# A graph network's edge table: zeroing and first scatters moved into the table stage, gathers paced otherwise

## The reference

```python
# attention: k, q, v per node by node type; per edge by edge type
a = (rel(k[src], rel_att, etype) * q[dst]).sum(-1) * rel_pri.T[etype] / sqrt(D)
ex = exp(a - segment_max(a, dst)[dst]);  attn = ex / segment_sum(ex, dst)[dst]
h = segment_sum(rel(v[src], rel_msg, etype) * attn, dst)
h = typed_linear(h, Wa, ntype) * gate + x * (1 - gate);  x = ln(x + ln(x + h) * gamma + beta)
# then three times, with the normalised weights norm of the edges:
h = x @ W;  agg = segment_sum(h[src] * norm, dst);  h = relu(batch_norm(agg + b))
```

## Time and profile before

| | |
|---|---|
| median of 3 runs | 4593.5 us (4591.87 to 4594.39) |
| the profiled execution | 4592.2 us, its span 4590.3 us |
| PE busy | 2969.0 us (65%) |
| DVE busy | 2312.5 us (50%) |
| POOL busy | 2411.3 us (53%) |
| ACT busy | 1147.0 us (25%) |
| table stage | start to about 405 us |
| attention, first gather to the last batch's logits less maxima (L1318) | 409 to 2168 us |
| first gather of the first convolution | 2595 us |

### The profile page before, as it was taken

One profiled execution on the slowest core, in us unless ns is written; L12 is line 12 of the kernel. 1 busy time (PEld: TensorE's weight loads), 2 busy tenths in 40 slices (PEclk: granted clock), 3 DMA queues, 4 the chain that ended last, 5 costly groups with the idle time before them and its releaser, 6 DMA issues. The chain is left out here.

```text
span 4590.3 us, 52237 instructions
## 1 busy us (share of the span) xinstructions
PE 2969.0 (65%) x14449; PEld 2143.5 (47%) x14449; DVE 2312.5 (50%) x8186; ACT 1147.0 (25%) x2512; POOL 2411.3 (53%) x2514
## 2 busy tenths in 40 slices
PE   3895666666676666664420666777767776767774
PEld 3774656666666656663200433344433444433342
DVE  3774655655655555553522345533455534455435
ACT  1223556555655555552001200000000000000001
POOL 0002544444466666665577266665466664666662
PEclk9998778777787877776755889988899988999987
DMA  4896555565422322221000455555545545555552
GB/s 110 273 358 232 199 200 210 189 216 191 163 88 80 87 79 81 84 81 48 1 1 0 172 190 174 189 191 184 186 174 190 189 174 179 192 188 176 189 189 61
DMA packets 232026, 706.47 MB, mean 154 GB/s; under 512 B 62326, under 2 KB 111957, under 8 KB 212928
## 3 DMA queue, kind: packets, MB, share of 16 engines
q1 hardware_dynamic: 104252, 447.79, 26.7%
q0 software_dynamic: 93184, 191.21, 14.4%
q10 hardware_dynamic: 34308, 64.13, 4.3%
HBM read 559.66 MB, written 143.28 MB: 153 GB/s over the span
## 5 line engine op out<-in xcount | busy, mean ns | idle before, releaser
L552 POOL DMA_INDIRECT stage<-h_tab,earr x1248 | 1183.3, 948 | 810.8 <-issue 346.5
L527 POOL DMA_INDIRECT arena<-kv_tab,idxr x832 | 796.0, 957 | 970.3 <-ACT idxr L634 405.6
L1013 PE MATMUL bank<-arena,xr 128*128 128x512 f32 (+1 forms) x2058 | 1021.1, 638 | 5.6 <-issue 5.6
L992 PE MATMUL bank<-oh,stage 128*128 128x128 f32 x2496 | 394.3, 308 | 494.0 <-issue 487.8
L992 PEld LDWEIGHTS bank<-oh,stage 128*128 128x128 f32 x2496 | 354.1, 214 | 712.3 <-issue 701.1
L860 PE MATMUL bank<-xr,arena 128*128 x3328 | 494.0, 308 | 236.8 <-DVE arena L1254 146.9
L1572 DVE TENSOR_TENSOR sums<-sums,bank 128x128 f32 x1248 | 351.3, 282 | 568.3 <-remote 398.2
L1013 PEld LDWEIGHTS bank<-arena,xr 128*128 128x128 f32 x2058 | 407.6, 212 | 394.8 <-issue 394.8
L860 PEld LDWEIGHTS bank<-xr,arena 128*128 128x128 f32 x3328 | 456.0, 218 | 259.3 <-issue 258.2
L499 POOL DMA_INDIRECT a_tab<-tot,cell x416 | 416.0, 1000 | 261.2 <-DMA arena<-kv_tab,idxr 151.1
L709 ACT ACTIVATE rs<-mv,epsc 128x49 f32<-128x49 f32 (+1 forms) x6 | 1.9, 316 | 2003.3 <-DVE mv L1611 1692.6
(11 more groups left out here) (224 smaller groups left out, 2739.4 us busy)
## 6 DMA issues: line engine op xcount, KB each, us to landing
arena<-a_tab SPq DMA_DIRECT2D x147, 1792.0 KB
a_tab<-stage SPq DMA_DIRECT2D x49, 1792.0 KB
kv_tab<-stage SPq DMA_DIRECT2D x48, 768.0 KB, 8.5
arena<-key_d ACTq DMA_DIRECT2D x52, 512.0 KB, 7.1
arena<-ew_d ACTq DMA_DIRECT2D x52, 512.0 KB, 10.1
arena<-rel_d SPq DMA_DIRECT2D x52, 512.0 KB
stage<-h_tab,earr POOLq DMA_INDIRECT x1248
arena<-kv_tab,idxr POOLq DMA_INDIRECT x832
```

The source lines that it names most:

```text
L527: G.indirect_dma_start(kv[b % 3][:, t, :], None, kv_tab, bass.IndirectOffsetOnAxis(idxr[:, b % 3, t:t + 1], 0))\
L552: G.indirect_dma_start(gring[:, (q % NG) * GRP + s, :], None, h_tab[l], bass.IndirectOffsetOnAxis(src_i[:, t:t + 1], 0)).then_inc(row_land ...
L992: last = M.matmul(bank[q % NG][:, s * P:(s + 1) * P], gring[:, (q % NG) * GRP + s, :], oh[:, q % NG, s, :], start=True, stop=True)
L1013: mm = M.matmul(o_[:, 0:cw], xr[:, n, :], abuf[B % NBUF][:, n % KB, 0:cw], start=n == 0, stop=n == NT - 1)
```

## The change

`a_tab` is zeroed by POOL in the table stage, from `hd`, a zeroed buffer of the sums that the attention needs later: 49 DMAs with rows of 14,336 bytes, released over the first 30 of the 49 node tiles. Then POOL waits for all zeros and issues the first 140 scatters; before every fourth it waits for all earlier ones to have landed. Only then does it wait for `tabs_complete` and begin to gather. SP's zero writes and the scatters between the gathers are gone. After the attention, 48 scatters come as before, then 228 instead of 224. The waits between gathers are changed: each group, the first of a batch too, waits for three of the four DMAs of the group before it (48), and for the fourth of the group before that (`kv_last`). DVE waits for the zeros before it clears `exw`.

```diff
+ZT = 30
+ST = 140
-                if b == 1:
-                    sp.wait_ge(zero_set, 2)
-                if b >= 1:
-                    for z in range(zeros_by(b - 1), zeros_by(b)):
-                        sp.dma_start(a_flat[z, :, :].rearrange("p (a f) -> p a f", a=4),
-                                     zero.rearrange("p (a f) -> p a f", a=1).to_broadcast([P, 4, ZW]))\
-                          .then_inc(a_zeroed[z // BPC], 16)
...
+            pool.wait_ge(zero_set, 1)
+            for z in range(NBLK):
+                if z:
+                    pool.wait_ge(kv_copied, z * ZT // NBLK)
+                G.dma_start(a_flat[z, :, :], hd[:, 0:KB * 512]).then_inc(a_zeroed[z // BPC], 16)
+            for j in range(ND):
+                pool.wait_ge(a_zeroed[j], 16 * BPC)
+            pool.wait_ge(cell_ready, 1)
+            for t in range(ST):
+                if t % GRP == 0:
+                    pool.wait_ge(cells_saved, 16 * t)
+                    pool.wait_ge(tot_added, KT * (t // KT + 1))
+                scatter(t)
             pool.wait_ge(tabs_complete, 1)
...
                 for g in range(NG):
-                    if g:
-                        pool.wait_ge(kv_land[b % 3][g - 1], 64 * (b // 3 + 1))
-                    for t in slots.get((b, g), ()):
-                        scatter(t)
+                    n = NG * b + g
+                    if n:
+                        b_, g_ = (n - 1) // NG, (n - 1) % NG
+                        pool.wait_ge(kv_land[b_ % 3][g_], 48 * (b_ // 3 + 1))
+                    if n >= 2:
+                        pool.wait_ge(kv_last[n % 2], 16 * (n // 2))
...
-                         .then_inc(kv_land[b % 3][g], 16)
+                         .then_inc(kv_land[b % 3][g] if s < GRP - 1 else kv_last[n % 2], 16)
...
-            V.memset(zero, 0.0).then_inc(zero_set, 1)
+            dve.sem_inc(zero_set, 1)
+            for j in range(ND):
+                dve.wait_ge(a_zeroed[j], 16 * BPC)
             V.memset(exw[:, :, :], 0.0).then_inc(exw_zero, 1)
```

More of the change, by code:

```diff
@@ L98, in gnn @@
     assert NT % KB == 0 and 2 * T1 == ET and T1 <= 512 and 512 * (ND - 1) < WD and WA + TPB <= 512 * ND and GT % GRP == 0
-    assert HALF + WD <= NW and T1 % KT == 0 and zeros_by(SB - 3) == NBLK
+    assert HALF + WD <= NW and T1 % KT == 0
     def groups_before(d):
@@ L247, in gnn @@
         a_zeroed = [sem(f"a_zeroed{j}") for j in range(ND)]
-        ZW = KB * 512 // 4
-        zero = stage[:, :, :, :].rearrange("p a r f -> p (a r f)")[:, TPB * P:TPB * P + ZW]
         edge_saved = [sem(f"edge_saved{a}") for a in range(2)]
@@ L263, in gnn @@
         kv_land = [[sem(f"kv_land{a}_{g}") for g in range(NG)] for a in range(3)]
+        kv_last = [sem(f"kv_last{a}") for a in range(2)]
         rel_in = [sem(f"rel_in{a}") for a in range(2)]
@@ L500, in scatter @@
                  .then_inc(cells_saved, 16)
-            pool.wait_ge(tabs_complete, 1)
[L504 to L508, removed]
+            pool.wait_ge(zero_set, 1)
[11 more added lines that the diff above has]
+                scatter(t)
+            pool.wait_ge(tabs_complete, 1)
             def gather(b):
@@ L528, in gather @@
                                              bass.IndirectOffsetOnAxis(idxr[:, b % 3, t:t + 1], 0))\
-                         .then_inc(kv_land[b % 3][g], 16)
+                         .then_inc(kv_land[b % 3][g] if s < GRP - 1 else kv_last[n % 2], 16)
             for b in range(NB):
                 gather(b)
-            for t in range(first_of, first_of + SY):
+            pool.wait_ge(tot_ready, 1)
+            for t in range(ST, ST + SY):
                 scatter(t)
@@ L537, in _ @@
             G.tensor_tensor(xr[:, :, :], xr[:, :, :], lnw[:, 1:2, :].to_broadcast([P, NT, D]), ALU.add).then_inc(xb_ready, 1)
-            for t in range(first_of + SY, T1):
+            for t in range(ST + SY, T1):
                 scatter(t)
@@ L632, in indices @@
                     for g in range(NG):
-                        act.wait_ge(kv_land[b % 3][g], 64 * (b // 3))
+                        act.wait_ge(kv_land[b % 3][g], 48 * (b // 3))
+                    for a in range(2):
+                        act.wait_ge(kv_last[a], 16 * (NG // 2) * (b - 2))
                 S.activation(idxr[:, b % 3, :], idx_c[:, bass.ds(b * TPB, TPB)], ACT.Copy).then_inc(idx_ready, 1)
@@ L1238, in _ @@
             dve.wait_ge(tabs_complete, 1)
[L1239 removed]
+            dve.sem_inc(zero_set, 1)
+            for j in range(ND):
+                dve.wait_ge(a_zeroed[j], 16 * BPC)
             V.memset(exw[:, :, :], 0.0).then_inc(exw_zero, 1)
             def products(b, i, par, g):
[L1244 removed]
+                dve.wait_ge(kv_land[b % 3][g], 48 * (b // 3 + 1))
+                dve.wait_ge(kv_last[g % 2], 16 * ((NG * b + g) // 2 + 1))
                 dve.wait_ge(q_done, NG * b + g + 1)
```

5 lines of the change are left out of this document (removed).

## The result

The changed kernel is a little slower: 4606.1 us median of 13 runs (4592.7 to 4621.4) against 4590.5 of the kernel before (13 runs, 4580.3 to 4594.9), a ratio of 1.003 with a 95% interval of 1.0021 to 1.004. Two later measurements gave 1.0043 (1.0019 to 1.0066) and 1.0033 (1.0019 to 1.0047). The profiled execution of the changed kernel took 4592.7 us, span 4591.0; it is the shortest of its 13. The forecast was 4505.

What follows compares the result with a forecast made beforehand. POOL's gathers and their landing waits were taken to bound the attention. A gain of 409 us there less 321 us lost before the first gather gave -88 us on 4592.2, so 4505 us; range 4425 to 4625.

Steps and rivals of the forecast that it cites:

- What bounds before: Attention of the kernel before: POOL bounds, sixteen gathers and three landing pauses making 27.1 us a plain batch.
- Part 1: Attention: without zeros and scatters, batches fall from 31.85 and 33.78 to 27.05 us, 277 us off POOL's path.
- Part 2: Attention: shorter waits between gathers bring a batch to 24.7 us; the attention gains 409 us in all.
- The pace: POOL's gathers in the attention: a group takes 6.07 us, all four of a batch 24.3 us.
- The three loops: Attention: the batch loops of DVE, ACT and POOL lie between 23.3 and 24.5 us, so 24.7 a batch.
- First batch: Start of the attention: 54.3 us less 6 for four shorter groups, 48 us.
- Last batch: End of the attention: 75.6 us before; its unexplained excess of 41.9 us over a batch is kept, giving 66.6.
- Part 3: Table stage: the zeros land at 455 us, the 29th tile copy comes at 443, the stage ends at 585 instead of 405.
- Part 4: Before the first gather: 140 scatters, 10 us a group beside full queues, then 6.6; first gather at 730, 321 us lost.
- Part 5: The rest of the kernel: SP's dropped DMAs and four more late scatters change nothing; all that follows shifts as it is.
- Rival 1: Attention: hand-offs between DVE, ACT and PE hold a batch at 27.05 us; gain 290 against 321 lost, 4625 us; chance 0.14.
- Rival 4: Attention: a batch takes 24.0 us and the last batch's stall goes, 4428 us; chance 0.08.

Runs made afterwards that it cites:

- e1: The changed kernel with the old waits between gathers (all four of the group before, none before a batch's first group): 4359.4 us, 1.0047 of before.
- e4: The changed kernel with the 48 scatters behind the last gather issued in fours, each after the landing of the earlier ones: 4311.4 us, 0.9939 of before.
- g2: The changed kernel with its 48 tail scatters in fours, without the gathers of batches 3 to 51 and the waits for them: 4412.2 us (one run).
- g4: The changed kernel unedited, run again beside a before of 4569.4 us: 4585.1 us, 1.0033 of before.
- after: The changed kernel as it is: 4606.1 us, 1.003 of before.
- f2: The changed kernel with its 48 tail scatters in fours and waits for all four gathers in the first three batches: 4586.9 us, 0.9992 of before.
- f1: The changed kernel with its 48 tail scatters in fours (the program of e4), beside a before of 4589.9 us: 4563.9 us, 0.9949 of before.
- g3: The kernel before with only its last 48 scatters issued in fours, each after the landing of the four before: 4534.1 us, 0.9929 of before.
- g1: The changed kernel with its 48 tail scatters in fours and groups waiting for two of four gathers, not three: 4966.7 us, 1.0873 of before.

## Why the prediction was wrong

The direction was wrong, by one term: the 24.7 us a batch, which were 25.6. Taken in the prediction's order:

- **What bounds before.** Right. POOL's pauses set 27.05 us a plain batch; e1 has 27.3 with the old waits and nothing else.
- **Part 1** (27.05 a batch without zeros and scatters). Right by e1.
- **Part 2, 24.7 us a batch. This step failed.** It stood on two terms, and both were too small.
  - The pace: "With the same 3.57 us it releases the next group". Most groups did (6.0 to 6.2 us), but one in six took over 7.2, so a batch of gathers takes 25.9 to 26.2 us instead of 24.3. I took one timeline of one group, with none of SP's loads beside it, for the mean. On kind B the same waits took a batch from 27.3 (e1) to 26.2 (e4).
  - The three loops: "between 23.3 and 24.5". They take 23.4 in g2, but only without POOL. Beside its gathers they take 25.0 to 25.7 on kind A (g4, after) while POOL has a lead. That they would need the same beside denser gathers was assumed without a reason.
  - Which of the two binds differs. In the profiled changed kernel it is the loops: DVE waits once, for 0.7 us, for gathered rows between 840 and 2060 us. In g4 it is first the loops and then the pace, on kind B the pace. Either alone keeps a batch at 25 us or more.
  - The missing 86 us can be put down either way, not both. By POOL's queue they are 52 batches of 1.6 us. By the other engines they are 25 in the first batch, 44 in the next 49 and 18 in the last two. A kernel near its sum's zero can't bear that: 409 earned against 321 paid left 88.
- **First batch**, 48: it took 73.1 on kind A and 43 on kind B. POOL's gathers go on meanwhile; f2 took the 20 us out by slowing POOL, and ended later.
- **Last batch.** "I have no cause for it; those scatters stand in the same place after, so I keep the excess." The excess stayed, and its cause on kind A was that row of 48 scatters (f1, g3). On kind B the same row costs nothing (17.0 us in e1).
- **Part 3.** Right: 29th tile copy 442.4 (443), first scatter 465.1 (455), last tile copy 578.9. The Trainium skill (DMA: Bandwidth & Descriptors, Specifications) gives 358 GB/s as the limit of device memory for a core; two slices of the page are above it, at 413 and 403, and the stretch from 75 to 470 us has 361. The trace doesn't bear it out as a limit for this kernel, and the measured packet prices were the better guide. The same page of the Trainium skill (Bandwidth, Measured) gives this figure for two cores of a pair that stream at once and 425 GB/s for one alone; this kernel runs on one core, and what the other did isn't on record.
- **Part 4.** Right in sum: first gather 740.9 (730), thirteen groups of 8.1 to 11.8 us beside full DMA queues, 10.4 on average (10), and mostly 6.2 where DMA is idle (6.6). Two of them, the gap ahead of each:

```profile
540.53 0.96 POOL L489 DMA_INDIRECT a_tab<-tot,cell  x1 [5.46 <-DMA a_tab<-tot,cell]
```

```profile
671.30 0.96 POOL L489 DMA_INDIRECT a_tab<-tot,cell  x1 [1.43 <-DMA a_tab<-tot,cell]
```

- **Part 5.** Nearly right: the rest of the kernel came 8.5 us shorter.
- **Rival 1** was the near one. It had the pace at 27.05 and 4625 us; it came to 25.9. Its point of decision was given as 26.5 us a batch, but that was reckoned by the batches alone. By POOL's pace it lies near 26: 24.3 plus 88/52. Its reason, the hand-offs by themselves, was wrong (g2). Rival 4's other half, that the last batch's stall goes, did not come: on kind A that needs the 48 scatters spread (f1), not the other 140 moved.

## What to carry to other kernels

A pause that looks like waste on a queue can be what lets another engine work. Before taking pauses out, look for an engine whose instructions come slowly with nothing to wait for while the queue's row is close, and try the row in both densities. And a period that is multiplied by fifty must come from the mean of many groups, not from one timeline, and must be read beside what the other queues move once in each period: here 1 to 1.6 us a batch turned a gain of 2% into none.

## What the runs showed of the hardware

- On kind A TensorE's matmuls come 0.7 or 1.4 us apart instead of 0.11 while GpSimd issues indirect DMAs about 1.26 us apart in a row; in the last batch it began 4.4 us after the start of such a row (2085.0 us). Pauses of 1.3 us in each group of four let it run nearly freely (25.0 to 25.7 us a batch against 23.4 without gathers); pauses of 0.8 with rows of five or six did not (44 us). What PE signals also comes late there: 1.6 us after the matmul at the median in the changed kernel and up to 46 us in its last batch, against 0.04 without gathers (g2) and on kind B (e4). DVE and ACT showed no slowness of their own, only waits: the mean of an instruction is 0.37 and 0.45 us in g1 as in g2. What in the chip does this wasn't found.
- Two chips show little of it and run the same kernel before in 4333 to 4339 us instead of 4569 to 4590; one program was 0.962 of before on the one kind and 1.047 on the other. About 220 of those 250 us lie behind the attention (2179 to 2200 us from the last L1319 to the end, against 2400 to 2435). No experiment was made there, but it has the same mark: the matmuls between POOL's gathers (L992) stand for 487.8 us with nothing named in before, and for 195.1 in e4.
- Landings of gathers aren't uniform. In the changed kernel a group with packets of SP's queue beside it releases the next after 6.9 us on average (7.3 in e4), another after 6.3, with a median of 6.1. That SP's loads are the cause is likely and not shown; a quarter of the late groups have none of them.
